# The sign sums t1 and n4 on GpSimd, and a new order of the work up to the second pair of row tiles, in a gated cross-attention and binarised linear kernel

## What is computed

```python
def _layernorm(x, axis=-1, eps=1e-05):
    m = jnp.mean(x, axis=axis, keepdims=True)
    v = jnp.var(x, axis=axis, keepdims=True)
    return (x - m) / jnp.sqrt(v + eps)
...
a = jnp.einsum('bqd,bkd->bqk', query, key)
e = jax.nn.softmax(a, axis=-1)
c = jnp.einsum('bqk,bkd->bqd', e, key)
...
alpha = jnp.mean(jnp.abs(W), axis=tuple(range(1, W.ndim)), keepdims=True)
return alpha * jnp.sign(W)
...
x = x + jnp.tanh(g_xattn[0]) * _L0_xattn_ref(_layernorm(x, axis=-1), ctx_4096)
x = x + jnp.tanh(g_ffn[0]) * _L0_ffn_ref(_layernorm(x, axis=-1), L0_ffn_weight_real, L0_ffn_bias)
```

## Time and profile before

| | |
|---|---|
| median of 3 runs | 1012.34 us (1010.96 to 1014.2) |
| the profiled execution: its own time | 1012.6 us |
| its span from first to last instruction | 1010.8 us |
| mean granted TensorE clock | 0.981 of full speed |
| TensorE (PE) busy | 941.6 us, 93% |
| VectorE (DVE) busy | 870.4 us, 86% |
| ScalarE (ACT) busy | 563.7 us, 56% |
| GpSimd (POOL) busy | 149.8 us, 15% |

### The profile page before, as it was taken

How to read it: one execution, slowest core, us unless ns; L and a number is a source line. 1 busy time by engine, 2 the same in 40 slices (tenths; PEclk the granted TensorE clock), 3 DMA queues, 4 the chain that set the end, 5 groups by cost and what they waited for, 6 DMA issues and landing times.

```text
span 1010.8 us, 14224 instructions
## 1 busy us (share of the span) xinstructions
PE 941.6 (93%) x5201; PEld 464.3 (46%) x5201; DVE 870.4 (86%) x1213; ACT 563.7 (56%) x617; POOL 149.8 (15%) x268
## 2 busy tenths in 40 slices
PE   2659999899999799999999899999999899999998
PEld 2435554444444344444444444444444444444443
DVE  6788999799989989897989989898989989897834
ACT  5999851545567574735557473735567473742310
POOL 0111022301112120202011120302011120302000
PEclk9779999899999899999999999999999999999999
DMA  9879718657887989796796988687797869674552
GB/s 311 270 223 240 205 22 219 178 104 170 171 198 172 226 167 227 132 201 170 164 217 121 242 172 214 143 195 173 157 215 137 239 120 214 157 162 102 112 125 83
DMA packets 365140, 178.66 MB, mean 177 GB/s; under 512 B 353424, under 2 KB 353424, under 8 KB 354448
## 3 DMA queue, kind: packets, MB, share of 16 engines
q1 hardware_dynamic: 365072, 177.76, 74.9%
HBM read 55.58 MB, written 33.55 MB: 88 GB/s over the span
## 4 chain that ended last, share of the span: by engine, by line
PE 56%; issue 17%; DVE 16%; POOL 4%; ACT 3%; DMA 2%; SPq 0%; POOLq 0%; ACTq 0%; DVEq 0%
PE y_ps L1930 46%; PE s_ps L1862 4%; PE c_ps L1878 4%; DVE natural L1157 3%; PE y_ps L1898 2%; DVE xr L1233 2%; DMA xr<-in_x_dram 2%; DVE xr L1365 2%; ACT xn_q L763 1%; DVE snap_a L1275 1%; DVE xr L1278 1%; DVE snap_a L1272 1%; DVE st L1236 1%; POOL nm L631 1%; POOL ve L639 1%
## 5 line engine op out<-in xcount | busy, mean ns | idle before, releaser
L1930 PE MATMUL y_ps<-wsign,ring_a 128*128 128x512 fp8e4 x1792 | 407.0, 380 | 0.0
L1930 PEld LDWEIGHTS y_ps<-wsign,ring_a 128*128 128x128 f16 x1792 | 174.4, 98 | 208.5 <-issue 2.1
L1930 PE MATMUL y_ps<-spare,ring_a 128*128 128x512 fp8e4 x896 | 198.9, 379 | 0.7 <-ACT snap_b L880 0.7
L1930 PEld LDWEIGHTS y_ps<-spare,ring_a 128*128 128x128 f16 x896 | 86.9, 98 | 105.3 <-ACT snap_b L880 1.7
L1233 DVE SCALAR_TENSOR_TENSOR xr<-c_ps,coef,xr 128x512 f32<-128x512 f32 x128 | 95.5, 746 | 26.0 <-PE c_ps L1878 25.6
L763 ACT ACTIVATE xn_q<-xr,nm,r 128x1024 f32<-128x1024 f32 x62 | 76.9, 1241 | 56.8 <-DVE natural L1157 35.4
L747 ACT ACTIVATE natural<-xn_a 128x1024 f16<-128x1024 f32 x76 | 79.2, 1053 | 44.7 <-DVE xn_a L1378 34.6
L1930 PE MATMUL y_ps<-sg,ring_a 128*128 128x512 fp8e4 x448 | 99.4, 379 | 0.0
L1157 DVE TENSOR_TENSOR natural<-xn_a,natural 128x1024 f16<-128x1024 f32 x78 | 94.7, 1216 | 4.7 <-ACT natural L747 4.7
L1878 PE MATMUL c_ps<-kd,pt 128*128 128x512 f16 x256 | 80.7, 398 | 13.8 <-DVE xr L1233 10.9
L1236 DVE BATCH_NORM_STATS2 st<-xr 128x6 f32<-128x512 f32 x128 | 88.9, 694 | 4.4
(11 more groups left out here) (116 smaller groups left out, 1012.3 us busy)
## 6 DMA issues: line engine op xcount, KB each, us to landing
xr<-in_x_dram SPq DMA_DIRECT2D x32, 1024.0 KB, 5.9
out_dram<-xr SPq DMA_DIRECT2D x30, 1024.0 KB, 4.6
spare<-n_L_ffn_weight_real_dram SPq DMA_DIRECT2D x8, 1024.0 KB, 6.1
ctx_f<-in_ctx_dram SPq DMA_DIRECT2D x8, 512.0 KB, 7.3
xr<-n_L_ffn_weight_real_dram SPq DMA_DIRECT2D x4, 1024.0 KB, 7.4
ctx_f<-n_L_ffn_weight_real_dram SPq DMA_DIRECT2D x4, 1024.0 KB, 6.8
out_dram<-xr SPq DMA_DIRECT2D x8, 256.0 KB, 2.2
ring_a<-natural SPq DMA_TRANSPOSE x102, 4.4
```

What stands on the lines that cost most here:

```text
L1930: last = nc.tensor.matmul(y_ps[:, BANKS[j] + n, :], ring_a[:, slot_a(p, j), part, k, :], RIGHT[j][:, k // 2, chunk(n), k % 2], start=(firs ...
```

## The change

`make_t1` and `make_n4` become GpSimd instructions with the same operands and the same waits; `make_t2` and `make_t3` stay on VectorE. The written order is another one on all five engines up to the loop over the pairs; the loop itself is as before, and so is every other operation. `scale1(u)` on GpSimd now calls `rstd1(u)` for u from 3 on.

```diff
             def scale1(u):
+                if u >= DVE_LN1:
+                    rstd1(u)
+                    return
...
+            def make_t1(n):
+                pool.wait_ge(out_act, turn("w", 2 * (2 + n) + 1) + 1)
+                pool.wait_ge(out_dve, turn("w", 2 * (2 + n) + 1) + 1)
+                pool.wait_ge(w_signed, 13)
+                wait_abs(pool, 12)
+                cols = chunk(n)
+                nc.gpsimd.tensor_tensor(t1[:, :, cols], b12[:, :, cols], b11[:, :, cols], ALU.subtract,
+                                        saturate=False).then_inc(t1_set, 1)
+
+            def make_n4(n):
+                pool.wait_ge(t2_set, n + 1)
+                pool.wait_ge(turn_tr, 2 * turn("w", NW // 2 - 1) + 2)
+                cols = chunk(n)
+                nc.gpsimd.tensor_tensor(n4[:, :, cols], b21[:, :, cols], t2[:, :, cols], ALU.subtract,
+                                        saturate=False).then_inc(n4_set, 1)
...
             mean_1(4)
-            rstd1(4)
+            scale1(4)
+            make_t1(0)
             mean_1(5)
-            rstd1(5)
+            make_t1(1)
+            scale1(5)
             scale2(3)
...
             reduce_keys(1)
+            make_n4(0)
             mean_1(8)
+            rstd1(8)
+            make_n4(1)
             scale2(6)
-            rstd1(8)
...
-            def make_t1(n):
-                dve.wait_ge(out_act, turn("w", 2 * (2 + n) + 1) + 1)
...
-                nc.vector.tensor_tensor(t1[:, :, cols], b12[:, :, cols], b11[:, :, cols], ALU.subtract,
...
-                nc.vector.tensor_tensor(n4[:, :, cols], b21[:, :, cols], t2[:, :, cols], ALU.subtract,
...
             take_keys(1)
-            sum_abs(2)
...
+            split_probs(0)
+            sum_abs(2)
             attention(0, 0)
...
-            make_n4(0)
             attention(5, 0)
-            make_n4(1)
+            make_t2(1)
+            finish_y(2, 3)
             low_q(6, 0)
...
```

More of the change, by code:

```diff
@@ L475, in _ @@
             turn_q(5, 0)
+            load_keys(1)
             turn_q(5, 1)
@@ L667, in _ @@
             mean_1(3)
-            rstd1(3)
+            scale1(3)
             scale2(1)
@@ L1473, in _ @@
             attention(2, 2)
[L1474 removed]
             low_q(3, 1)
             attention(2, 3)
+            scale_bias()
+            sum_abs(8)
+            add_bias(0)
+            spread_alpha(5)
+            low_x1(2, 0)
+            take_w(4)
+            low_x1(2, 1)
             add_bias(1)
+            max_logits(3)
             spread_alpha(6)
[L1479 to L1481 removed]
+            split_probs(3)
+            spread_alpha(7)
             finish_y(0, 0)
[L1483 removed]
@@ L1484, in _ @@
-            max_logits(3)
+            add_bias(2)
             take_alpha(1)
-            split_probs(3)
             spread_alpha(8)
-            low_x1(2, 1)
-            add_bias(2)
             spread_alpha(9)
+            finish_y(1, 0)
+            spread_alpha(10)
+            sum_abs(11)
             take_w(5)
-            sum_abs(11)
-            attention(3, 0)
+            finish_y(0, 1)
             low_q(4, 0)
-            spread_alpha(10)
-            finish_y(1, 0)
-            attention(3, 1)
@@ L1568, in _ @@
             low_a(0, "S2")
+            make_t3(1)
+            max_logits(7)
+            make_s4(0)
+            low_a(0, "S1")
             split_probs(7)
-            add_bias(5)
             attention(6, 3)
-            low_a(0, "S1")
             attention(7, 0)
-            low_a(0, "A22")
-            make_s4(0)
             attention(7, 1)
-            finish_pair(0, "C11", 0)
-            low_a(0, "S4")
             attention(7, 2)
             key_scales(1)
+            attention(7, 3)
+            low_a(0, "S4")
+            add_bias(5)
+            low_keys(1)
+            finish_pair(0, "C11", 0)
             low_q(8, 0)
@@ L1600, in _ @@
-            make_s2(1)
-            low_q(9, 0)
-            attention(8, 0)
-            low_a(1, "S2")
-            add_bias(7)
-            low_q(9, 1)
-            finish_pair(1, "C11", 0)
-            low_a(1, "S1")
+            low_a(1, "S2")
+            low_q(9, 1)
+            add_bias(7)
+            low_a(1, "S1")
+            finish_pair(1, "C11", 0)
+            finish_pair(1, "C11", 1)
+            attention(8, 0)
+            make_s4(1)
+            low_a(1, "A22")
+            max_logits(9)
@@ L1608, in _ @@
             attention(8, 1)
-            make_s4(1)
-            finish_pair(1, "C11", 1)
+            split_probs(9)
             attention(8, 2)
-            max_logits(9)
-            low_a(1, "A22")
-            split_probs(9)
             attention(8, 3)
             low_q(10, 0)
+            low_q(10, 1)
             attention(9, 0)
-            low_q(10, 1)
+            low_a(1, "S4")
             attention(9, 1)
+            attention(9, 2)
             finish_pair(1, "C22", 0)
-            low_a(1, "S4")
```

367 lines of the change are left out of this document (172 added, 195 removed), and 4 rows, old and new, of the table NAT.

## The result

The changed kernel takes **1024.81 us** (median of 4 runs, 1024.62 to 1026.21), the kernel before beside it 1011.74 (4 runs, 1010.96 to 1014.2): a ratio of 1.012 with a 95% interval of 1.0105 to 1.0134. It is slower, as forecast, but by 13 us where 4.3 were forecast, and 0.8 us beyond the range. Its profiled execution took 1024.62 us with a span of 1022.7.

What follows compares the result with a forecast made beforehand. It took VectorE's lateness, which leaves TensorE gaps ahead of 336 us, as the bound. Terms -5.0 + 16.0 - 4.4 - 2.3 = +4.3 us on a median of 1012.3 gave 1016.6 us, range 1001 to 1024.

Steps and rivals of the forecast that it cites:

- Price of a sum: Time of one t1 or n4 sum on GpSimd: 8.0 us, ends 3.2 and 9.4.
- Start: Up to 90 us, mostly reorderings; the absolute sum moves behind the first softmax: -1 us, ends -2.3 and +2.
- t1 (0) covered: First half of t1 on GpSimd runs beside three VectorE attention chunks that it cannot hold: cost 0, ends 0 and +4.
- t1 (1): Second half of t1, directly ahead of `rstd1(5)` on GpSimd, delays `low_q(5, 0)` to about 138.5: +1.6 us, ends 0 and +4.
- First gap gone: TensorE's 3.15 us gap and 2.4 of slow clock vanish; with earlier terms `attention(5, 3)` comes 5.0 us earlier.
- `reduce_keys` and n4 (0) at about 210: On GpSimd, `reduce_keys(1)` with two preparations takes 14.1 us, putting n4 (0) at about 210.
- n4, +16.0 less 4.4: Each n4 half on GpSimd holds VectorE for 8.0 us, +16.0 (ends 0 and 18.8); idle time absorbs 4.4.
- rival B: n4 (1) falls beside five attention chunks, covering 7 of its 8.0 us: -2.7 us, 1009.6; chance 0.19.
- Tail: `add_bias(9)` moves behind `split_probs(11)`, for which TensorE waits to 335.68: -2.3 us.
- DMA queue: `load_keys(1)` moves ahead, `store(2)` and `load_x(8)` back, each waiting for finished work: cost 0, ends -1 and +2.
- A (no hold): VectorE's two-operand instructions run on beside a GpSimd sum, so the 16.0 go: -11.7 us, 1000.6; chance 0.25.
- C: n4 (1) ends too late for TensorE's product A22, so the full 18.8 is paid: +11.5 us, 1023.8; chance 0.13.

Runs made afterwards that it cites:

- after_n4free: The changed kernel with n4 left out, all but one column that GpSimd writes, t1 on GpSimd: 1016.56 us, ratio 1.0025.
- before_n4free: The kernel before, own order and t1 on VectorE, with n4 left out, all but one column that GpSimd writes: 1008.3 us, ratio 0.9953.
- move_t1: The kernel before in its own order, only t1 moved to GpSimd, n4 left on VectorE: 1014.65 us, ratio 1.0008.
- order_only: The changed kernel with its whole new order, but the four sums t1 and n4 made by VectorE again: 1024.36 us, ratio 1.0105.
- after_cover: The changed kernel with GpSimd's n4 (0) ahead of the key maximum, waiting for low part A12: 1019.6 us, ratio 1.0056.

## Why the prediction was right in sign and wrong in size

- **Price of a sum**: 8.0 taken, 7.47 measured; within the ends.
- **Start** (-1): TensorE's first product with weight signs began at 76.28 against 75.78, so +0.5; within its ends, of the other sign.
- **t1 (0) covered**: right, nothing is held beside it. **t1 (1)**, +1.6: right in place, too small; `low_q(5, 0)` came at 140.49 (forecast 138.5), 3.6 us late and within the ends. And one small instruction was held for 4.5 us, which the step did not have.
- **First gap gone, -5.0 at `attention(5, 3)`**: right; 190.83, which is 4.75 earlier.
- **`reduce_keys` and n4 (0) at about 210**: right; 13.5 us with both preparations, start at 212.01.
- **n4, +16.0 less 4.4**: the mechanism was right, the size not. The hold works both ways, but the new order puts the last of tile 6's three attention chunks and a step that reads `y_ps` beside the first 3 us of n4 (0), so that VectorE is held for 4.4 us, and three chunks of tile 7 beside n4 (1), which holds nothing. Price 7.2 instead of 11.6 at the marker (9.6 by the times), most of it the first half's. That is rival B's mechanism for n4 (1), and my words that the chunks were already past failed for n4 (0). In the order before the price is 15.7 at the marker (13.2 by the times), not far from the 16.0. The 4.4 that idle time was to absorb was a choice; no run measures it.
- **Tail, -2.3**: this is the step that failed. It priced one moved `add_bias` and left the rest of the new order at nothing. From tile 5's last chunk to the marker, with n4 left out, the new order goes from -5.0 to +1.8: **+6.8 instead of -2.3** (+7.5 if the marker is replaced by the time of after_n4free). `add_bias(9)` did move; TensorE's wait of 7.71 us fell to 4.53, with a new one of 2.10 ahead of it.
- **DMA queue, 0**: one wait of 1.45 us on a turned part; it goes with the hold.

The sum by measured terms is -5.0 + 6.8 + 7.2 = +9.0 at the marker, where the forecast had -5.0 - 2.3 + 11.6 = +4.3. The two errors are +9.1 and -4.4 (by the times +9.8 and -2.0); the price of n4, set too high, hid part of the order's. The last 3 us were in no term: I had taken it that the kernel moves by as much as the loop's start does, and the loop of this profile took 2.9 more.

**Rivals.** A (no hold) fell. B's cover came true for n4 (1), its time did not. C's time was nearly hit, its mechanism was not: TensorE waits ahead of A22 for ScalarE's copy, and n4 (1) had ended 13.6 us earlier (240.85 + 7.48 against 261.94). That C's time came so close is luck. That the new order itself loses was no rival, and it is half of the result.

Open: which of the many moved steps costs the 4.7 us behind the softmax of tile 6. The chunks that stand together are not it by themselves. Between that softmax and the marker TensorE idles 13.8 us in after_n4free and 11.1 in before_n4free, and it is busy 1.9 us longer with the same work (16 matmuls behind its last long gap take 5.92 us against 4.53): part of the 4.7 is the clock.

## What to carry to other kernels

When a change moves work and rewrites the order around it, price the order by itself: the cheapest test is the new order with the work left where it was, and one with the work left out. Work given to an engine that can hold another costs what it holds, so look at which instructions lie beside it and put it beside those that read elsewhere; one moved call with one wait did this here for 0.6% of the time. Such a cover is bought with an order, and the order cost more (8.1 us) than the work was worth (6.3).

## What the runs showed of the hardware

**The hold, in the other direction.** The earlier trace rows show VectorE's sums holding GpSimd. A GpSimd sum of 7.47 us that reads two SBUF operands held VectorE instructions with two SBUF operands to its end (7.96 for 1.2, 6.64 and 5.07 for 0.69). It let pass those with an operand in PSUM (0.67, 0.75), the chunk statistics (0.69), and, beside t1 (1), a reduction of 64 columns (0.22) and a step on one column (0.21). My forecast had no place for the `prob` row, 4.66 for 0.19 us: it reads one SBUF tile of 64 fp32 columns (in move_t1 another of that kind, 128 columns, took 2.77 for 0.28). The Trainium skill (SBUF — State Buffer, who interferes with whom) puts VectorE's two-port modes beside the two-operand reads as what contends; the trace agrees that two SBUF operands aren't the only case, with 4.66 us. In which mode that row ran, no run shows.

**The same gap, another clock.** TensorE has two gaps of 3.45 us in the steady loop in both kernels, ended by the same step. Behind the first, TensorE's timeline of the kernel before:

```profile
565.87 0.23 PE L1869 MATMUL s_ps<-ident,prob 128*128 128x128 f16 x1 [3.45 <-DVE prob L1222]
...
566.40 3.62 PE L1930 MATMUL y_ps<-wsign,ring_a 128*128 128x512 fp8e4 x16
```

and of the changed one:

```profile
574.85 0.23 PE L1872 MATMUL s_ps<-ident,prob 128*128 128x128 f16 x1 [3.45 <-DVE prob L1245]
...
575.38 5.30 PE L1933 MATMUL y_ps<-wsign,ring_a 128*128 128x512 fp8e4 x16
```

Before, the 16 matmuls run at the upper level, 2.4 GHz (226 ns each; granted clock 1.00 from 565.87 to 570.10). After, with the same 3.45 us of idling ahead, they run partly at the lower one, 1.2 GHz (331 ns on average; granted clock 0.71 from 574.85 to 580.70), 1.7 us more; behind the second gap they take 3.61 and 4.54 us. Where I read the loop, these stretches make up the steps of the rest in the table: none in the kernel before (617.0), 1.0 us in after_n4free (618.4), 2.6 in the changed kernel (620.0), 4.2 in order_only (621.7). That is probably also why the kernel before itself spread from 1010.6 to 1017.6 us over all comparisons (mean granted clock 0.981 in the fastest of these runs, 0.971 in the slowest); its other runs weren't traced. The sharpest pair is the 2.20 us gap of after_n4free (ended at 203.16) and of after_cover (203.19): the same step, 0.03 us apart, and the 16 matmuls behind it take 3.62 us at a granted clock of 1.00 and 5.30 at 0.68. So a single profile compares two orders to no better than some 3 us; the marker tells where time goes, the interval how much.
